# Weighted experts of a pair on partition halves, four banks for the first W1 blocks, experts' input by GpSimd

## What is computed

```
x = x + graph_mix(group_norm(x))                 # channels to 64 nodes, 9 edge types, back
t = tokens(x)                                    # 16 x 256 x 64
t = t + ssm(layer_norm(t))                       # gated scan over 256 steps an image, 128 x 16 states
t = t + moe(layer_norm(t))                       # below
moe(t): xn = layer_norm(t)
        top 2 of softmax(t @ Wr + br) out of 8 experts, their weights divided by their sum
        y_e = gelu(xn @ W1[e] + b1[e]) @ W2[e] + b2[e]      # 64 -> 256 -> 64
        out = sum over the two chosen e of weight_e * y_e
```

## Time and profile before

| | |
|---|---|
| median of 3 runs | 400.85 us (400.56 to 401.72) |
| the profiled execution's own time | 402.59 us |
| its span, first to last instruction | 400.9 us |
| PE busy, instructions | 337.8 us (84%), 1658 |
| DVE busy, instructions | 330.0 us (82%), 454 |
| ACT busy, instructions | 280.1 us (70%), 458 |
| POOL busy, instructions | 265.9 us (66%), 270 |
| granted TensorE clock, mean | 0.944 of 2.4 GHz |

### The profile page before, as it was taken

The page is one execution under the profiler, slowest core; times in us unless marked ns, Lnnn a source line. Parts: engine busy times, 40 slices in busy tenths (PEclk is TensorE's granted clock), DMA queues, the critical chain, the costliest instruction groups (busy, mean ns, idle before and its releaser), DMA issues. The chain is left out here.

```text
span 400.9 us, 5477 instructions
## 1 busy us (share of the span) xinstructions
PE 337.8 (84%) x1658; PEld 183.1 (46%) x1658; DVE 330.0 (82%) x454; ACT 280.1 (70%) x458; POOL 265.9 (66%) x270
## 2 busy tenths in 40 slices
PE   0597896677899889989998898899889877999794
PEld 0484445333455345444544453455245425555452
DVE  2774457997899999999999999999999988994411
ACT  1002667488968997898799869987987757761472
POOL 8706112986579966994899589858985994692122
PEclk9996999588999999998999999999989986999899
DMA  8771079899899698659975897589758960000000
GB/s 196 211 146 19 0 191 222 214 222 227 206 229 217 149 213 205 155 147 212 206 165 133 199 234 164 137 191 222 166 150 194 222 141 1 2 0 15 1 0 13
DMA packets 21236, 59.52 MB, mean 148 GB/s; under 512 B 4924, under 2 KB 13272, under 8 KB 15320
## 3 DMA queue, kind: packets, MB, share of 16 engines
q1 hardware_dynamic: 20040, 58.34, 63.4%
q10 hardware_dynamic: 1168, 0.84, 0.9%
HBM read 53.93 MB, written 5.24 MB: 148 GB/s over the span
## 5 line engine op out<-in xcount | busy, mean ns | idle before, releaser
L347 POOL TENSOR_TENSOR hs<-hs,Cs 128x1024 f32<-128x1024 f32 x63 | 149.3, 2373 | 42.8 <-DVE hs L769 42.2
L769 DVE TENSOR_TENSOR_SCAN hs<-av,P 128x1024 f32<-128x1024 f32 x64 | 146.3, 2286 | 4.7 <-PE P L1056 1.3
L635 ACT ACTIVATE hb<-P,b1c 128x512 f32<-128x512 f32 x128 | 81.5, 683 | 18.6 <-PE P L1179 16.3
L762 DVE SCALAR_TENSOR_TENSOR P<-P,bbcol,ub 128x1024 f32<-128x1024 f32 x62 | 79.7, 1285 | 2.4 <-DMA ub<-u_scratch 1.1
L1192 PE MATMUL P<-hb,W2s 128*64 128x256 f32 x512 | 69.3, 394 | 0.0
L1178 PE MATMUL P<-X,W1H 128*128 128x512 f32 x128 | 60.1, 469 | 5.6 <-ACT hb L635 4.4
L1179 PE MATMUL P<-X,W1L 128*128 128x512 f32 x128 | 52.6, 411 | 0.0
L578 ACT ACTIVATE av<-P,Aneg 128x510 f32<-128x510 f32 x68 | 44.1, 686 | 10.9 <-PE P L1131 6.9
L359 POOL TENSOR_TENSOR accs<-accs,mes 128x256 f32<-128x256 f32 x56 | 40.9, 730 | 14.1 <-DVE mes L860 9.5
L1192 PEld LDWEIGHTS P<-hb,W2s 128*64 128x64 f32 x512 | 31.6, 137 | 31.0 <-issue 21.1
L860 DVE SCALAR_TENSOR_TENSOR mes<-P,cols,wbs 128x256 f32<-128x256 f32 x64 | 27.3, 467 | 16.9 <-PE P L1192 9.6
(11 more groups left out here) (191 smaller groups left out, 478.8 us busy)
## 6 DMA issues: line engine op xcount, KB each, us to landing
ub<-u_scratch SPq DMA_DIRECT2D x31, 1024.0 KB, 10.8
av<-dt_scratch SPq DMA_DIRECT2D x15, 1024.0 KB, 7.4
dt_scratch<-dts SPq DMA_DIRECT2D x7, 256.0 KB, 2.8
u_scratch<-rl SPq DMA_DIRECT2D x7, 256.0 KB, 2.8
av<-in_L_conv_Wr SPq DMA_DIRECT2D x2, 576.0 KB, 6.9
av<-in_L_conv_Wl SPq DMA_DIRECT2D x2, 576.0 KB, 7.7
...
```

Of the source, the lines that this page charges most:

```text
L347: gp.tensor_tensor(hs[:, at, :, :], hs[:, at, :, :], rep(Cs[:, p, :], 1, 2), ALU.mult).then_inc(S["cm"], 1)
L635: a_.activation(hb[:, r % 4, :], P[:, (XA, XB)[r % 2], :], ACT.Gelu, bias=b1c[:, r:r + 1]).then_inc(S["gl"], 1)
L762: v.scalar_tensor_tensor(out=ring, in0=rep(P[:, BB, :], 1, 2), scalar=bbcol[:, 0:1], in1=ub[:, 2 * n:2 * n + 2, :], op0=ALU.add, op1=ALU.m ...
L769: v.tensor_tensor_scan(hs[:, (SLOTS * g + n) % RING].rearrange("p a t -> p (a t)"), av[:, 2 * n:2 * n + 2, :].rearrange("p a t -> p (a t)" ...
```

## The change

- **Experts' input.** GpSimd makes both parts of X2: a copy of `xnt2` in fp32r, then the difference, both ahead of slot 1's product. VectorE's two copies go (they remain for the last batch). The router's intermediate results lie in PSUM instead of `rt`; `dve_router1` stands in one piece.
- **W1 blocks.** `f1_bank` gives blocks 0 to 5 the banks XB, YS, XD, XA, XB, XD; four may be written before a gelu is done. The filler products ahead of the experts go. `pe_experts` lists the order: W2 products 0 to 3 one by one between blocks 4 to 7.
- **Partition halves.** A W2 product covers all 512 columns and goes to output partitions 0 to 63 for an even expert, 64 to 127 for an odd one. So a pair's weights are one product of 512 columns (`selW`, `wT` by 16 rows, four transposes instead of two), the weighting is one instruction of 128 x 512 a pair, with b2 in pairs, and GpSimd adds whole pairs (three sums of 512 columns a batch).
- **Fold.** The two halves are added by a product with `foldm` (two stacked identities) in the next body, behind W1 block 3; ScalarE copies the result (`act_folded`, between gelus 0 and 1), GpSimd adds it to `t1` behind slot 2 (`pool_out`), and the output is stored from `t1`, inside `sp_spread`. For the last batch TensorE folds `acc` and the last pair into one bank and VectorE adds.
- **Order.** VectorE weights pair 0 after slot 3, and pairs 1, 2, 3 after slots 4, 5, 6. ScalarE's `act_dhi` moves from behind gelu 1 to behind gelu 13.

The diff, cut (setup, renamed counters, and the last batch's list, which is the same `pe_experts`, are left out):

```diff
+        def f1_bank(r):
+            return (XB, YS, XD, XA, XB, XD)[r] if r < 6 else (XA, XB)[r % 2]
...
+        def sp_out(sp_, g, p):
+            sp_.wait_ge(S["fin"], g + 1)
+            for h in range(2):
+                sp_.dma_start(ov[h, :, g:g + 1, :], t1[64 * h:64 * h + 64, p:p + 1, :]).then_inc(S["out_sem"], 16)
...
+                if c == 1 and g >= 3:
+                    sp_out(sp_, g - 3, (g - 3) % 2)
...
+        def pool_acc(eng, g, j):
+            eng.wait_ge(S["me"], PAIRS * g + j + 1)
+            if j == 1:
+                since(eng, "fold", g)
+                prev = mes[:, 0, :]
             else:
-                eng.wait_ge(S["acc"], EXP * g + e)
-                prev = acc[:, p, :]
-            gp.tensor_tensor(acc[:, p, :], prev, mes[:, e % 4, :], ALU.add).then_inc(S["acc"], 1)
+                eng.wait_ge(S["acc"], 3 * g + j - 1)
+                prev = acc[:, :]
+            gp.tensor_tensor(acc[:, :], prev, mes[:, j % 2, :], ALU.add).then_inc(S["acc"], 1)
...
+        def pool_out(eng, g):
+            eng.wait_ge(S["ev"], g + 1)
+            eng.wait_ge(S["cen2"], g + 1)
+            gp.tensor_tensor(t1[:, g % 2, :], t1[:, g % 2, :], folded[:, :], ALU.add).then_inc(S["fin"], 1)
...
         def pool_x2(eng, g):
             eng.wait_ge(S["xn2"], 2 * (g + 1))
+            since(eng, "f1", EXP * KC * g)
+            gp.tensor_copy(X2[0:64, :], xnt2[:, :]).then_inc(S["xh2"], 2)
             eng.wait_ge(S["xh2"], 2 * (g + 1))
-            eng.wait_ge(S["cm"], min(SLOTS * (g + 1) + 2, SLOTS * G))
-            since(eng, "acc", EXP * g)
+            eng.wait_ge(S["cm"], SLOTS * (g + 1) + 1)
+            eng.wait_ge(S["u"], min(g + 3, G))
+            since(eng, "acc", 3 * g)
             gp.tensor_tensor(X2[64:128, :], xnt2[:, :], X2[0:64, :], ALU.subtract).then_inc(S["xl2"], 1)
+            eng.wait_ge(S["xl2"], g + 1)
...
+                if prev is not None:
+                    pool_x2(eng, prev)
                 pool_slot(eng, i, p, 1)
                 if prev is not None:
-                    pool_x2(eng, prev)
                     pool_router(eng, prev)
                 pool_slot(eng, i, p, 2)
+                if prev:
+                    pool_out(eng, prev - 1)
                 pool_slot(eng, i, p, 3)
                 pool_slot(eng, i, p, 4)
-                weighted(0)
+                weighted(1)
                 pool_slot(eng, i, p, 5)
                 weighted(2)
                 if nxt is not None:
...
                     if prev is not None:
...
                     pool_dlo(eng, nxt)
                     eng.wait_ge(S["dlo"], nxt + 1)
                 pool_slot(eng, i, p, 6)
...
-                weighted(4)
+                weighted(3)
...
+        def act_folded(eng, g):
+            eng.wait_ge(S["fold"], g + 1)
...
+            a_.activation(folded[:, :], P[:, XC, HW:T], ACT.Copy).then_inc(S["ev"], 1)
         def act_gelu(eng, g, p):
             for r in (2 * p, 2 * p + 1):
+                if r == 1 and g > 0:
+                    act_folded(eng, g - 1)
                 eng.wait_ge(S["f1"], EXP * KC * g + r + 1)
...
-                a_.activation(hb[:, r % 4, :], P[:, (XA, XB)[r % 2], :], ACT.Gelu, bias=b1c[:, r:r + 1]).then_inc(S["gl"], 1)
+                a_.activation(hb[:, r % 4, :], P[:, f1_bank(r), :], ACT.Gelu, bias=b1c[:, r:r + 1]).then_inc(S["gl"], 1)
...
-                        if n == 0 and nxt is not None:
-                            act_dhi(eng, nxt)
                         if n == 1:
                             act_wt(eng, prev)
                         if n in range(2, 6):
                             act_wb(eng, prev, n - 2)
+                        if n == 6 and nxt is not None:
+                            act_dhi(eng, nxt)
...
-            if between is not None:
-                between()
+            if between is None:
+                return
+            between()
...
-            v.scalar_tensor_tensor(out=rt[:, 5], in0=rt[:, 4], scalar=-2.0, in1=chances, op0=ALU.mult, op1=ALU.add).then_inc(S["e2"], 1)
+            v.scalar_tensor_tensor(out=others, in0=rt[:, 4], scalar=-2.0, in1=chances, op0=ALU.mult, op1=ALU.add).then_inc(S["e2"], 1)
...
+        def dve_expert(eng, g, j):
+            eng.wait_ge(S["f2"], EXP * KC * g + 2 * KC * (j + 1))
+            eng.wait_ge(S["wb"], PAIRS * g + j + 1)
+            since(eng, "acc", 3 * g + (j >= 2))
+            v.scalar_tensor_tensor(out=mes[:, j % 2, :], in0=P[:, (XC, XD)[j % 2], :], scalar=cols[:, R["b2"] + j:R["b2"] + j + 1],
+                                   in1=rows_w[:, j, :], op0=ALU.add, op1=ALU.mult).then_inc(S["me"], 1)
...
                 dve_slot(eng, i, 3)
+                experts(0)
                 dve_slot(eng, i, 4)
-                experts(0)
+                experts(1)
                 dve_slot(eng, i, 5)
+                experts(2)
...
-                experts(2)
                 dve_slot(eng, i, 6)
-                experts(4)
+                experts(3)
                 dve_slot(eng, i, 7)
...
-                experts(6)
...
+            for j in range(PAIRS):
+                dve_expert(eng, G - 1, j)
+            eng.wait_ge(S["fold"], G)
+            eng.wait_ge(S["fin"], G - 1)
+            v.tensor_tensor(t1[:, (G - 1) % 2, :], P[:, YS, 0:HW], t1[:, (G - 1) % 2, :], ALU.add).then_inc(S["fin"], 1)
...
         def pe_wt(eng, g):
             eng.wait_ge(S["vlo"], g + 1)
-            eng.wait_ge(S["xn1"], so_far(g, 4))
-            since(eng, "me", EXP * g)
...
...
+            for h in range(2):
+                for q in range(2):
+                    at = HW * h + 128 * q
+                    pe.transpose(P[0:2 * EXP, YS, at:at + 128], vv[:, q, h].rearrange("p r e -> p (r e)"), ident[:, :]).then_inc(S["wtr"], 1)
...
-            for e in (2 * r, 2 * r + 1):
-                pe.matmul(P[:, YS, HW * (e % 2):HW * (e % 2) + HW], selW[:, e, :], wT[:, :],
-                          start=True, stop=True).then_inc(S["wb_mm"], 1)
+                eng.wait_ge(S["wb"], PAIRS * g + r)
+            pe.matmul(P[:, YS, :], selW[:, r, :], wT[:, :], start=True, stop=True).then_inc(S["wb_mm"], 1)
...
+        def pe_fold(eng, g):
+            eng.wait_ge(S["acc"], 3 * g + 3)
+            eng.wait_ge(S["o2"], g + 2)
+            for h in range(2):
+                last = pe.matmul(P[64 * h:64 * h + 64, XC, HW:T], foldm[:, :], acc[:, HW * h:HW * h + HW], start=True, stop=True)
+            last.then_inc(S["fold"], 1)
...
+            eng.wait_ge(S["me"], PAIRS * (g + 1))
+            for h in range(2):
+                last = pe.matmul(P[64 * h:64 * h + 64, YS, 0:HW], foldm[:, :], mes[:, 1, HW * h:HW * h + HW], start=False, stop=True)
+            last.then_inc(S["fold"], 1)
...
         def pe_f1(eng, g, r):
             e, k = r // KC, r % KC
+            done = EXP * KC * g
             if r == 0:
                 eng.wait_ge(S["xl2"], g + 1)
+            if r == 1:
+                eng.wait_ge(S["aexp"], NBLK * so_far(g, 2) - 1)
+            if r == 2:
+                eng.wait_ge(S["xn1"], so_far(g, 4))
+                since(eng, "me", PAIRS * g)
+            if r == 3:
                 eng.wait_ge(S["sp_relu"], so_far(g, 2))
                 eng.wait_ge(S["aexp"], NBLK * so_far(g, 2))
-            if r >= 2:
-                eng.wait_ge(S["gl"], EXP * KC * g + r - 1)
-            bank = (XA, XB)[r % 2]
+            if r >= 4:
+                eng.wait_ge(S["gl"], done + (1, 3, 4, 5)[r - 4] if r < 8 else done + r - 1)
+            bank = f1_bank(r)
...
             if r == 0:
-                eng.wait_ge(S["e2"], g + 1)
+                eng.wait_ge(S["o2"], g + 1)
+                since(eng, "ev", g)
             if r == 2 * KC:
-                eng.wait_ge(S["wtc"], g + 1)
+                eng.wait_ge(S["gl"], EXP * KC * g + 6)
             if r % (2 * KC) == 0 and pair >= 2:
-                eng.wait_ge(S["me"], EXP * g + 2 * (pair - 1))
-            for h in range(2):
-                last = pe.matmul(P[64 * h:64 * h + 64, (XC, XD)[pair % 2], HW * (e % 2):HW * (e % 2) + HW], W2s[:, e, k, :],
-                                 hb[:, r % 4, HW * h:HW * h + HW], start=(k == 0), stop=(k == KC - 1))
-            last.then_inc(S["f2"], 1)
+                eng.wait_ge(S["me"], PAIRS * g + pair - 1)
+            at = 64 * (e % 2)
+            pe.matmul(P[at:at + 64, (XC, XD)[pair % 2], :], W2s[:, e, k, :], hb[:, r % 4, :],
+                      start=(k == 0), stop=(k == KC - 1)).then_inc(S["f2"], 1)
...
+        def pe_experts(eng, g):
+            for r in range(4):
+                pe_f1(eng, g, r)
+            if g > 0:
+                pe_fold(eng, g - 1)
+            pe_f1(eng, g, 4)
+            pe_f2(eng, g, 0)
+            pe_wt(eng, g)
+            pe_f2(eng, g, 1)
+            pe_f1(eng, g, 5)
+            pe_f2(eng, g, 2)
+            pe_f1(eng, g, 6)
+            pe_wb(eng, g, 0)
+            pe_f2(eng, g, 3)
+            pe_f1(eng, g, 7)
+            pe_f2(eng, g, 4)
```

(77 more changed lines are left out.)

88 lines of the change are left out of this document (40 added, 48 removed).

## The result

The changed kernel takes 464.44 us (median of 4, 463.12 to 466.16) against 400.71 us of the kernel before in the same job: 1.159 times, 95% interval 1.154 to 1.164. The profiled execution has 465.0 us with a span of 462.4, 61.5 longer than the 400.9 of before. The forecast was 460 us, 441 to 473.

What follows compares the result with a forecast made beforehand. VectorE (DVE) was taken as the bound, TensorE only just ready. Bodies 1 to 5 at 5.9 + 1.6 each (37.5), body 6, body 7 and the end gave +55.6; clock 3.4 made +59.0 on 400.85: 460 us, range 441 to 473.

Steps and rivals of the forecast that it cites:

- W2: TensorE's W2 products: without a neighbour in the other half they run one after another; +6.9 us, bounds 0 to +7.6.
- W1 blocks: TensorE after the first gelu: two W1 blocks fewer remain to be done; -0.9 us.
- weight rows: TensorE: one product of 512 columns replaces two of 256, four times; -0.8 us, bounds 0 and -1.2.
- transposes: TensorE: four transposes instead of two; +0.3 us, 0.2 to 0.6.
- alternation: TensorE: W2 products standing singly between W1 blocks, about four more changes; +0.4 us, 0 to 1.0.
- Expert order: From last W2 product to gate: last weighting now precedes slot 7, 7.95 us instead of 6.35; +1.6 us, 1.3 to 1.8.
- Experts' input: Copy and subtraction on GpSimd, VectorE's two copies gone: slot 1's product some 3.5 us late, off the path; 0.
- Body 6, body 7, the end: The last bodies and the end, priced separately from bodies 1 to 5: +5.95, +6.45 and +5.7 us.
- Clock, 3.4 us: TensorE idling over 2 us before the last sum may lower the clock in bodies 2 to 6; 0 to 6.8, half taken.
- 1 and 2: Rivals: long W2 products cheap as the pairs; 391 us (1), or gain lost in waits, 401 to 404 (2); chance 0.05 each.
- 3: Rival: PE serial as forecast, but slack absorbs part; 442 us, between 436 and 447; chance 0.08.
- 4: Rival: low clock in every expert stage too; 473 us, upper part of the forecast, which has chance 0.82 with it.

Runs made afterwards that it cites:

- split: The changed kernel with each W2 product of 512 columns cut into two of 256, both still into the expert's own half; 463.68 us, ratio 1.156.
- side: The changed kernel with W2 products ordered r, r + 2, r + 1, r + 3, so each stands beside one of the other half; 438.20 us, ratio 1.092.
- x2: The kernel before with GpSimd making both parts of the experts' input, VectorE's two copies gone and the router still in SBUF; 410.78 us, ratio 1.026.
- fill: The changed kernel with eight filler products on TensorE between the last W2 product and the product that writes B; 460.02 us, ratio 1.147.

## Why the prediction was right

The time lies in the range and the named mechanism was at work; that the total came within 5 us is partly luck, as two terms were off in opposite directions and the clock was taken by halving a bound. The gates, forecast 45 to 47 us apart, are 47.1 to 48.4.

- **W2, +6.9 us a body.** Right: 1.86 us for two r where 1.87 follows from 1.01 + 0.86, and `split` and `side` show that it is the neighbour. The four r that stand singly take 1.00 each to the next start, so all sixteen cost +7.0 in body 4 (15.2 us against 8.1).

```profile
250.27 1.07 PE L1251 MATMUL P<-hb,W2s 128*64 128x512 f32 x2
251.27 0.60 PE L1191 MATMUL P<-ident,vv 128*16 128x128 f32 x4
```

- **W1 blocks −0.9, weight rows −0.8, transposes +0.3, alternation +0.4.** The last W2 product ends 39.2 us after the gate (229.20 - 190.00; 39.0 in body 4) instead of 32.4: +6.8, where the sum was +5.9. The term that failed is the weight rows: 262.50 to 262.92 is 0.42 us, and it was 0.43 for the two short ones. So one product of 512 columns saves nothing over two of 256. With 0 for it the sum is 6.7. In body 4 the W1 blocks with their restarts give −0.7 (7.2 against 7.9), the transposes +0.2. The upper bound of the W2 term has a slip: 1.92 less 1.01 is 0.91, so it is +7.3 and not +7.6; the forecast doesn't use it.
- **Expert order, +1.6 us.** Right where the clock is full, by the chain that was named: 7.98 us against 7.95 (the terms as given add to 7.93), and 6.8 + 1.6 is the 8.4 us by which body 3 is longer (47.18 against 38.74 to 38.76). Not seen was the second chain, through the product of B, the step-size product and the four sums, which ends just behind it and takes over at the low clock. That is how two products at half speed come to cost 1.4 us: I had followed VectorE's and GpSimd's queues from the moved wait, and not TensorE's.
- **Experts' input, 0.** Nearly right in the changed kernel, where VectorE idles later and the 1.2 us of L876 reach TensorE's fold alone, and wrong as a price: alone the edit costs 10 us (`x2`). I had looked at who waits by semaphore. The trace of before holds one small sign that I passed over: in body 7 the operation that is L848 in `x2` (L843 here), 0.18 us in the bodies before, takes 0.29 and ends with GpSimd's subtraction (VectorE and GpSimd, timelines of before).

```profile
337.33 0.29 DVE L843 TENSOR_TENSOR rt<-rt,rv 128x32 f32<-128x32 f32 x1
```

```profile
336.31 1.26 POOL L372 TENSOR_TENSOR X<-xnt,X 64x512 fp32r<-64x512 f32 x1 [1.05 <-DVE X L815]
```

- **Body 6, body 7, the end.** +7.8, +5.6, +4.2 against 5.95, 6.45, 5.7 without the clock; together 17.6 against 18.1. Body 6 is split by `fill`: there its gates are 374.90 - 330.53 = 44.4 us apart, +5.9, and the other 1.9 us of the +7.8 go with a stretch at 0.51 in the seam, and belong to the clock term. Body 7 and the end came out shorter than forecast where the profiled execution of the kernel before has low stretches of its own, 10.2 us in body 7 and 3.4 in the end, and the changed one only 3.4 in body 7. That this is the whole difference is not shown. Stretches of the changed kernel (body 6), then of the kernel before (body 7):

```profile
370.50:377.00 6.50, 5.68 (x22) 1.50 (x26) 5.85 (x4) 2.81 (x5) 5.02 (x5) 0.51 0.37 95
```

```profile
335.40:342.20 6.80, 5.91 (x12) 3.31 (x13) 6.43 (x17) 5.10 (x8) 2.75 (x7) 0.50 0.00 0
```

- **Clock, 3.4 us.** `fill` gives 4.4. Of bodies 1 to 5 only two have it in the seam, by 1.4 us each against those of 47.0, not each of them; body 6 has it by 1.9. And I had counted only what is added: the low stretch behind the gate of body 1, priced at 1.36 us, is gone in the changed kernel (1.00 from 94 to 100 us).
- The rivals: 1 and 2 fall with the 1.86 us for two r; 3 (slack that absorbs part) has no trace, the gates were 47 apart; 4 is excluded by the profile of the changed kernel: in body 4 the clock is 1.00 from 246 to 278 us, over all experts, and of the later bodies only 7 has a low stretch in them.
